# Third scan in units of 1024 columns, with one pair of PSUM banks for each spread

## What is computed

```python
dt = softplus(dtr @ dt_w.T + dt_b)            # (32 sequences, 1024 pixels, 32 channels)
A = -exp(A_log)                               # 32 channels x 16 states
def step(h, inp):
    dt_t, B_t, C_t, x_t = inp
    dA = exp(dt_t[..., None] * A)
    h = dA * h + (dt_t * x_t)[..., None] * B_t[:, None, :]
    y = einsum('bds,bs->bd', h, C_t)
    return h, y
y = ys + xc * Dp
```

## Time and profile before

| | |
|---|---|
| median of 3 runs (lowest, highest) | 2015.61 us (2015.4, 2015.81) |
| profiled execution | 2014.68 us |
| its span, first to last instruction | 2012.7 us |
| mean granted TensorE clock | 0.942 |
| busy over the span: TensorE, VectorE, GpSimd, ScalarE | 82%, 79%, 58%, 58% |
| third scan, setup to last output | 1380.9 to 1909.4 us |
| s_ahead scan of 1024 columns (L1147), mean | 2287 ns |
| s_prod multiplication of 1024 columns (L1173), mean | 2439 ns |
| s_pfeed multiplication of 1024 columns (L1140), mean | 1233 ns |

### The profile page before, as it was taken

One profiled execution on the slowest core, in us unless ns is written; L12 is line 12 of the kernel. 1 busy time (PEld: TensorE's weight loads), 2 busy tenths in 40 slices (PEclk: granted clock), 3 DMA queues, 4 the chain that ended last, 5 costly groups with the idle time before them and its releaser, 6 DMA issues. The chain is left out here.

```text
span 2012.7 us, 31048 instructions
## 1 busy us (share of the span) xinstructions
PE 1651.0 (82%) x9878; PEld 979.8 (49%) x9878; DVE 1585.5 (79%) x1549; ACT 1158.2 (58%) x1889; POOL 1168.7 (58%) x881
## 2 busy tenths in 40 slices
PE   5888787996788888888888888657888888888787
PEld 2555444884444454444545544234555554554333
DVE  3788745554799999999999999441899999999854
ACT  3444484334666666666666665265666665665356
POOL 0666501001467767676776775202899999999701
PEclk8999988997899999999999999777999999999898
DMA  4000000000254444444444444200000000000001
GB/s 135 2 0 0 1 0 1 1 1 1 53 95 88 90 90 87 94 83 94 89 89 83 94 91 92 44 1 0 1 1 0 0 0 0 0 0 0 7 5 42
DMA packets 23435, 78.21 MB, mean 39 GB/s; under 512 B 3792, under 2 KB 4816, under 8 KB 23120
## 3 DMA queue, kind: packets, MB, share of 16 engines
q0 software_dynamic: 18432, 67.12, 17.6%
q1 hardware_dynamic: 4944, 10.35, 1.8%
HBM read 8.25 MB, written 2.10 MB: 5 GB/s over the span
## 5 line engine op out<-in xcount | busy, mean ns | idle before, releaser
L1173 POOL TENSOR_TENSOR s_prod<-s_ahead,s_cs 128x1024 f32<-128x1024 f32 x128 | 312.2, 2439 | 203.7 <-DVE s_back L1150 103.1
L1708 POOL TENSOR_TENSOR r_prod<-r_state,r_cs 128x512 f32<-128x512 f32 x256 | 322.4, 1298 | 14.8 <-DVE r_state L1649 14.2
L1147 DVE TENSOR_TENSOR_SCAN s_ahead<-s_fore,s_pfeed 128x1024 f32<-128x1024 f32 x128 | 292.7, 2287 | 11.8 <-ACT s_fore L1069 5.3
L1150 DVE TENSOR_TENSOR_SCAN s_back<-s_aft,s_pfeed 128x1024 f32<-128x1024 f32 x128 | 289.5, 2261 | 0.0
L1069 ACT ACTIVATE s_fore<-s_pd,s_aneg 128x896 f32<-128x896 f32 x128 | 129.7, 1013 | 161.0 <-PE s_pd L940 161.0
L940 PE MATMUL s_pu<-s_partsu,selr 128*128 128x512 f32 x512 | 173.4, 462 | 52.2 <-DVE s_pfeed L1140 52.0
L1636 DVE TENSOR_TENSOR r_feed<-r_pu,r_bs 128x512 f32<-128x512 f32 x256 | 164.4, 687 | 61.9 <-PE r_pu L1478 61.9
L1140 DVE TENSOR_TENSOR s_pfeed<-s_pu,s_bs 128x1024 f32<-128x1024 f32 x128 | 157.8, 1233 | 37.7 <-PE s_pu L940 25.0
L1601 ACT ACTIVATE r_decay<-r_pd,r_aneg 128x512 f32<-128x512 f32 x256 | 168.3, 686 | 23.2 <-PE r_pd L1478 23.0
L1478 PE MATMUL r_pu<-r_parts,selr 128*128 128x512 f32 x512 | 161.3, 437 | 5.7 <-DVE r_feed L1636 5.7
L1649 DVE TENSOR_TENSOR_SCAN r_state<-r_decay,r_carry,r_feed 128x512 f32<-128x512 f32 x128 | 156.3, 1263 | 0.0
(11 more groups left out here) (255 smaller groups left out, 3338.1 us busy)
## 6 DMA issues: line engine op xcount, KB each, us to landing
s_ahead<-s_back POOLq DMA_DIRECT2D x128, 512.0 KB, 4.5
x_act<-in_x_dram SPq DMA_DIRECT2D x8, 256.0 KB, 5.4
out_dram<-x_act SPq DMA_DIRECT2D x16, 128.0 KB, 2.3
k_scan<-in_pack_scan_dram SPq DMA_DIRECT2D x1, 1600.0 KB, 10.4
k_fir<-in_pack_fir_dram SPq DMA_DIRECT2D x1, 1600.0 KB, 13.8
k_l<-in_pack_l_dram SPq DMA_DIRECT2D x1, 450.0 KB, 6.9
k_ln<-in_pack_ln_dram SPq DMA_DIRECT2D x3, 131.0 KB, 3.0
k_mlp<-in_pack_mlp_dram SPq DMA_DIRECT2D x2, 194.0 KB, 5.1
```

Source lines behind the costliest of these rows:

```text
L1147: dve.tensor_tensor_scan(ahead[:, v % 4], f, feed[:], 0.0, ALU.mult, ALU.add).then_inc(ahead_done, 1)
L1150: dve.tensor_tensor_scan(back[:, v % 4, ::-1], a[:, ::-1], feed[:, ::-1], 0.0, ALU.mult, ALU.add).then_inc(back_done, 1)
L1173: pool.tensor_tensor(prod[:, b], ahead[:, v % 4], cs[:, buf].rearrange("p i n -> p (i n)"), ALU.mult).then_inc(prod_done, 1)
L1708: pool.tensor_tensor(prod[:, v % 2, q], state[:, v % 2, q], cs[:, v % UNROLL // 4, q], ALU.mult).then_inc(multiplied, 1)
```

## The change

The third scan runs in 128 units of 1024 columns, a whole sequence each, so nothing is carried. Sixteen units make one block of 1024 columns: `cells(u)` gives the first eight (phase 0) the quarters 0 and 2 in turn, the next eight (phase 1) the quarters 1 and 3. Preparation still goes by 512 columns, one such block every eight units (k = u % 8), and a unit needs both halves of its 1024 columns prepared; the lags become 11 (B and C), 15 (decays), 16 (inputs), 17 (scan), 18 (multiplication), 19 (y), 20 (its copy out). The loop is written out 32 at a time, with 32 ahead and 32 behind.

`ps_d`, `ps_u` and `feed` are now one pair of banks each. TensorE issues the four spreads of the inputs of one unit and the four of the decays of the next mixed, behind both waits. The low part of B and C is made by a matmul with the negative identity into `ps_m` and a ScalarE copy. `Dp * xc` comes from two fp32 matmuls with `place` into `ps_y` per eight units, and ScalarE copies `ps_y` back to `xc` in four pieces of 32 partitions. The product with C overwrites `state` (four buffers), which y reads, so a scan waits for the y of four units before (`wait(dve, y_part, p - 3)`). "grown" moves from GpSimd to ScalarE.

```diff
-        LAG_B, LAG_D, LAG_U, LAG_Y = 2, 5, 6, 7
+        LAG_B, LAG_E, LAG_D, LAG_A, LAG_P, LAG_Y, LAG_V = 11, 15, 16, 17, 18, 19, 20
-        ps_d, ps_u, feed = m.banks("r_pd", 2), m.banks("r_pu", 2), m.banks("r_feed", 2)
+        ps_d, ps_u, feed = (m.banks("r_p" + t, 1, (P, 2 * N))[0] for t in ("d", "u", "feed"))
```

TensorE:

```diff
+                k, par, gi = u % 8, u // 16, s - u % 8
+                if k == 2 and live(s, UNITS):
+                    at = slice(u % 16 // 8 * N, (u % 16 // 8 + 1) * N)
+                    pe.wait_ge(hi_bc, gi + 8)
+                    pe.matmul(ps_m[:], negid[:], parts_bc[:, par, 0, at], start=False, stop=True,
+                              skip_group_check=True).then_inc(bc_rest, 8)
+                p, e = s - LAG_D, s - LAG_E
...
+                    wait(pe, fed, p)
+                    jobs.append((ps_u, parts_u[:, half], q, g))
...
+                    wait(pe, decayed, e)
+                    jobs.append((ps_d, parts_d[:, half], q, g))
+                for chunk in range(2):
+                    for part in range(2):
+                        for bank, parts, q, g in jobs:
...
+                w = s - LAG_B
...
+                    wait(pe, s_copied, w)
+                    if k == 1 and live(s, UNITS):
+                        pe.wait_ge(relu_done, gi + 8)
+                    if k == 2 and live(s, UNITS):
+                        pe.wait_ge(lo_bc, gi + 8)
...
+                    mm.then_inc(s_rep, 1)
+                o, z = s - LAG_Y, (u - LAG_Y) % UNROLL3
+                if z % 2 == 1 and live(o, UNITS):
+                    _, phase, _, g = cells(z)
+                    if z % 8 == 1:
+                        wait(pe, y_done, o - 1)
+                        for chunk in range(2):
+                            pe.matmul(ps_y[:], place[:, 2 * phase + chunk],
+                                      xc[:, columns(o - z % 16 + 8 * chunk, N)], start=(chunk == 0), stop=False,
+                                      skip_group_check=True)
+                    pe.wait_ge(multiplied, o + 1)
...
+                    mm.then_inc(y_part, 2)
+                if k < 2 and live(s, UNITS):
+                    if live(w, UNITS):
+                        pe.wait_ge(s_copied, w + 1)
+                    if k == 0:
+                        wait(pe, lo_bc, gi)
+                        pe.matmul(ps_m[:], wdt[:], xc[:, columns(gi, N)], start=True, stop=True).then_inc(dt_ps, 8)
                     else:
+                        pe.wait_ge(relu_done, gi + 8)
+                        pe.matmul(ps_m[:], c["wbc"], xc[:, columns(gi, N)], start=True, stop=True).then_inc(bc_ps, 8)
```

ScalarE (within a unit: eviction of y, low part of B and C, decay, copy of B or C, then the preparation):

```diff
+                if z % 8 == 7 and live(o, UNITS):
+                    phase = z % 16 // 8
+                    act.wait_ge(y_part, o + 1)
+                    for chunk in range(2):
+                        for q in (phase, phase + 2):
+                            rows, src = slice(q * 32, q * 32 + 32), (q ^ chunk) * 32
+                            done = act.activation(xc[rows, columns(o - z % 16 + 8 * chunk, N)], ps_y[src:src + 32],
+                                                  ACT.Copy)
+                    done.then_inc(y_done, 8)
...
+                    act.activation(parts_bc[:, par, 1, at], ps_m[:], ACT.Copy).then_inc(lo_bc, 8)
...
+                    act.activation(decay[:, v % 4], ps_d[:], ACT.Exp, scale=aneg[:, g:g + 1]).then_inc(decayed, 1)
...
+                    act.activation(parts_bc[:, par, 0, at], ps_m[:], ACT.Copy).then_inc(hi_bc, 8)
...
+                    act.activation(one[:], one[:], ACT.Copy, bias=-1.0).then_inc(grown_done, 8)
```

VectorE:

```diff
+                    dve.wait_ge(u_rep, p + 1)
...
+                    wait(dve, scanned, p)
+                    dve.tensor_tensor(feed[:], ps_u[:], bs[:, phase, q // 2], ALU.mult).then_inc(fed, 1)
+                    dve.wait_ge(fed, p + 1)
+                    dve.wait_ge(decayed, p + 1)
+                    wait(dve, y_part, p - 3)
+                    dve.tensor_tensor_scan(state[:, v % 4], decay[:, v % 4], feed[:], 0.0, ALU.mult,
+                                           ALU.add).then_inc(scanned, 1)
```

More of the change, by code:

```diff
@@ L1425, in _, with skewed3 @@
                 pool.tensor_tensor(resid[:, cols], out[:, cols], x[:, cols], ALU.add).then_inc(resid_done, 1)
+UNROLL3, PEEL3 = 32, 32
+def skewed3(eng, body):
+    for s in range(PEEL3):
+        body(s, s)
+    with eng.Fori(0, (UNITS - PEEL3) // UNROLL3) as r:
+        for u in range(UNROLL3):
+            body(r * UNROLL3 + (PEEL3 + u), u)
+    for s in range(UNITS, UNITS + PEEL3):
+        body(s, s % UNROLL3)
 def scan3(nc, consts, xc, selr, ysel):
@@ L1435, in scan3 @@
         c, const_in = consts["l3"]
[L1436 to L1442, removed]
@@ L1443, in scan3 @@
[L1443 to L1451 removed]
+        wdt, place, negid = m.sb("r_wdtb", [P, P]), m.sb("r_place", [P, 4, P]), m.sb("r_negid", [P, P], F32R)
@@ new lines, in scan3 @@
+        delta, du, ex, one, ln = (m.sb("r_" + t, [P, N]) for t in ("delta", "du", "ex", "one", "ln"))
+        parts_d, parts_u, parts_bc = (m.sb("r_parts" + t, [P, 2, 2, 2 * N], F32R) for t in ("d", "u", "bc"))
+        decay, state = (m.sb("r_" + t, [P, 4, 2 * N]) for t in ("decay", "state"))
+        bs, cs = (m.sb("r_" + t, [P, 2, 2, 2 * N]) for t in ("bs", "cs"))
+        ps_d, ps_u, feed = (m.banks("r_p" + t, 1, (P, 2 * N))[0] for t in ("d", "u", "feed"))
+        ps_m, ps_y = (m.banks("r_p" + t, 1)[0] for t in "my")
@@ L1469, in _, with columns @@
+        def columns(first, width):
+            if isinstance(first, int):
+                return slice(first * 64, first * 64 + width)
+            return ds(first * 64, width)
         @block.tensor
@@ L1474, in _ @@
             pe.wait_ge(w_done, 1)
[L1476 to L1480, removed]
-            def body(s, u):
[L1483 to L1515, removed]
-                    else:
[L1517 to L1546, removed]
@@ L1571, in body @@
[L1571 to L1581, removed]
@@ new lines, in body @@
+                if not live(s, UNITS):
+                    return
+                if k == 0:
+                    act.wait_ge(dt_ps, gi + 8)
+                    wait(act, delta_done, gi)
+                    act.activation(ex[:], ps_m[:], ACT.Abs, bias=c["dtb"]).then_inc(away_done, 8)
+                    wait(act, du_done, gi)
+                    wait(act, hi_d, gi)
+                    wait(act, lo_d, gi)
+                    act.activation(delta[:], ps_m[:], ACT.Relu, bias=c["dtb"]).then_inc(relu_done, 8)
+                    act.wait_ge(away_done, gi + 8)
+                    act.activation(ex[:], ex[:], ACT.Exp, scale=-1.0).then_inc(ex_done, 8)
@@ L1660, in body @@
[L1660 to L1668 removed]
+                p, v = s - LAG_A, u - LAG_A
@@ new lines, in body @@
+                if not live(s, UNITS):
+                    return
+                if k == 3:
+                    pool.wait_ge(grown_done, gi + 8)
+                    pool.tensor_tensor(ex[:], ex[:], one[:], ALU.subtract).then_inc(off_done, 8)
+                    pool.wait_ge(off_done, gi + 8)
+                    pool.wait_ge(ln_done, gi + 8)
+                    pool.tensor_tensor(ex[:], ln[:], ex[:], ALU.add).then_inc(log_done, 8)
+                    pool.wait_ge(log_done, gi + 8)
+                    pool.wait_ge(relu_done, gi + 8)
+                    pool.tensor_tensor(delta[:], delta[:], ex[:], ALU.add).then_inc(delta_done, 8)
```

259 lines of the change are left out of this document (122 added, 137 removed).

## The result

The changed kernel takes 2113.45 us (median of four runs, 2112.26 to 2114.69) against 2015.71 of the kernel before on the same chip: ratio 1.0485, 95% interval 1.0471 to 1.0498. It is slower by 98 us; 64 were forecast, and the range ended at 2112, 1.5 us short.

What follows compares the result with a forecast made beforehand. GpSimd was taken as the old bound (30.8 us a block); the new period was VectorE's 29.2 plus stalls, 35.2 us. With 63.5 for the loop and 2.6 for the tail, 2014.7 became 2080.8, taken as 2080 us, range 2045 to 2112.

Steps and rivals of the forecast that it cites:

- The bound before, and the engines' sums: Third scan's loop: GpSimd bound at 30.8 us a block; new sums VectorE 29.2, GpSimd 27.2, TensorE 25.9, ScalarE some 21.
- the tail: From the end of the last scan: 6.9 us instead of 4.3, plus 2.6.
- The chain of k = 0 to 4: Waits through a block's first five units: stalls 0.65 + 2.1 + 0.4 + 0.8 + 2.0, period 35.2 us instead of 30.8.
- The clock: TensorE's rest from 16.4 to 19.1 in k = 3; a possible fall to 1.2 GHz was left out of the sum.
- The sum: Loop 14 x 35.2 plus 62, together 555 us, plus 63.5 over before; with tail 2.6, 2080.8 us.
- the first feed: Start of the third scan's loop: within 3 us of the old 1414, counted as nothing.
- The range: Whole kernel: 2045 to 2112 us, leaving out the faster rival, most of the half-hidden one and half of the clock's.
- the clock rival: TensorE at 1.2 GHz behind the k = 3 rest: 2.5 us a block, 35 in 14, 2115 us; chance 0.17.
- the list of waits: Waits between engines through one block, k = 0 to 7; GpSimd was said to stay inside and be level by k = 7.
- Banks: Skill's rule on rotating PSUM banks: by it the loss of the second bank counts; no size given, unused in the sum.
- The page on the clock: Skill page on kernels swinging between clock levels: cited for TensorE; old loop's first quarter said to agree, the rest not.

Runs made afterwards that it cites:

- The last run: B and C spreads and copies moved to k = 3 to 7 and 0, against the reordered kernel with evictions behind the decay and skip matmuls apart: 2005.55 us, ratio 0.9954.
- the new order: Changed kernel with TensorE issuing inputs, B or C, decays, then y, and ScalarE copying before the decay (k = 2 differs): 2062.09 us, ratio 1.0232.

## Why the prediction missed, step by step
- **The bound before, and the engines' sums.** Right: GpSimd's 27.2 us a block are 26.4, VectorE's share is 28.2 busy, a decay of 1024 columns 1.115 (1.12 estimated), four evictions 2.39 (2.3), two skip matmuls 1.88 with the pipe's depth (1.7), the tail 6.9.
- **The chain of k = 0 to 4.** Right in its places and its order, too short by 0.8 us a block, 10 us in 13 blocks. The clean measure is the run with all rests filled: 7.2 us of stalls against 6.0. Small hand-overs were left out at each step, such as 0.16 before the scan at k = 0 and 0.58 instead of 0.3 behind y at k = 2.
- **The clock.** This is the step that failed. "TensorE rests from 16.4 to 19.1 in k = 3" was seen, but the sum puts the fall behind it at nothing: it stood as a rival with 0.17, to decide only "if the rest lasts 3 us or more", with the old loop as evidence that such rests often pass. Here the rest was 2.58 us, and the granted clock fell in 13 of 14 blocks. It cost 1.6 us each, 21 us; 35 us was the rival's price.
- **The sum.** From the 2080.8 us of the forecast to the 2114.5 of the profiled execution it is 33.7 us: 21 by the clock, 10 by the chain, 2.4 by the first feed (given as nothing, within 3), 0.9 ahead of the stage; the first block was 1.0 shorter than forecast, and some tenths are left. That the total came within 2 us of the rival's 2115 is partly chance: its clock term was too large by about as much as the rest of the sum was too short.
- **The range.** It cut the clock rival in half, at 2112. With a chain whose every step can only be late and a rest of nearly that length in each block, the high end should have taken it in whole.
- **The copy of C** was missing from the list of waits. It cost nothing in the changed kernel, and made the bound of 30.9 us a block once the other waits were mended.
- **Banks.** By Perfetto Trace Analysis of the Trainium skill, Optimizing Tensor Performance, independent groups should rotate through banks. The last run shows that it decides nothing here: with one pair each, scans wait 5.4 us in all for a decay or for y between 1430 and 1850 us, never over 0.3 at once, and no feed waits, if the order leaves each hand-over its time.
- **The page on the clock.** TensorE: Matmul & The Clock Gate of the Trainium skill, "A second HAM failure mode: psum-queue depth-cycling", agrees with the traces better than I credited it: a TensorE that stops between groups went between 1.2 and 2.4 GHz in 13 of 14 blocks of the changed kernel. In the old loop the low stretches aren't in the first quarter alone, as the prediction has it; the trace shows two more near the end, at about 1885 and 1900 us.

Open: why the clock fell in only four of the last thirteen blocks with the evictions moved, and in five of thirteen without skip matmuls. Only filling the rests, or the new order, kept it at 1.0; in those runs TensorE's longest single wait in the loop is 1.3 us. Shorter rests were no guarantee elsewhere (1.3 and 0.8 us ahead of the fall at k = 2), and one of 2.6 us passed; which rest counts in which block the runs don't tell. Not tested either is whether a second pair of banks would have hidden the waits of the first order.

## What to carry to other kernels
Fewer busy microseconds on each engine say nothing when every buffer is single: write out one period of the loop, with each in-order engine's waits, and look for work that stands between a wait and something others wait for. Moving such work (copies ahead of the decay, evictions behind it, skip matmuls to the idle units) brought 108 us here, where the change itself had lost 98. And if the written-out period shows TensorE at rest for some two microseconds, price its lower clock into the forecast, not into the tail of the range.

## What the hardware showed that I had not expected
The low clock moved rather than went when one of two rests was filled: 2113 us with four idle spreads at k = 4, 2096 with ten at both places. Work that computes nothing made the kernel 17 us faster. And the price of one fall is much the same wherever it lands: 1.6 us at k = 4 in the changed kernel, 1.5 at k = 2 with the evictions moved, and 3.1 in the blocks without skip matmuls, where it falls at both.
